# Causal attention on one core: tile 1's mask moved from VectorE to TensorE, and two more PSUM banks for the scores once the last row maxima are out

## What is computed

```python
q, k, v = split(einsum('bsd,ed->bse', x, W_qkv)); q, k = rope(q), rope(k)
scores = where(causal, einsum('bhqd,bhkd->bhqk', q, k) / sqrt(8), -inf)
x = layernorm(x + einsum('bsd,ed->bse', softmax(scores) @ v, W_o))
w = quantize_int4(kernel)                      # round(w / scale), clipped to -8..7, times scale
x = layernorm(x + x @ w + bias + (x @ a) @ b)
```

## Time and profile before

| | us |
|---|---|
| median of 3 runs | 483.12 |
| lowest, highest | 478.73, 485.3 |
| the profiled execution | 482.48 |
| its span, first to last instruction | 480.7 |
| around the span | 1.8 |
| TensorE busy (matmul) | 444.2 |
| VectorE busy | 396.8 |
| ScalarE busy | 311.4 |
| GpSimd busy | 108.1 |
| mean granted TensorE clock | 0.955 |

### The profile page before, as it was taken

How to read it: one execution, slowest core, us unless ns; L and a number is a source line. 1 busy time by engine, 2 the same in 40 slices (tenths; PEclk the granted TensorE clock), 3 DMA queues, 4 the chain that set the end, 5 groups by cost and what they waited for, 6 DMA issues and landing times.

```text
span 480.7 us, 8224 instructions
## 1 busy us (share of the span) xinstructions
PE 444.2 (92%) x2914; PEld 200.1 (42%) x2914; DVE 396.8 (83%) x827; ACT 311.4 (65%) x630; POOL 108.1 (22%) x178
## 2 busy tenths in 40 slices
PE   4988799699799999999999999999999999999972
PEld 2445454334343344343434543434344434434542
DVE  1789689789989999999889999998999989933466
ACT  2324467278067868778778786767786788689610
POOL 8543511201100030020303311030002002442343
PEclk9999879899969999999999999999999999999975
DMA  7322211110000001110000011100000000000001
GB/s 240 143 89 89 91 39 54 54 54 24 3 0 2 1 14 55 55 54 14 3 2 3 14 55 55 54 11 1 1 2 3 1 3 2 3 24 1 22 1 44
DMA packets 11576, 16.54 MB, mean 34 GB/s; under 512 B 1820, under 2 KB 6700, under 8 KB 11536
## 3 DMA queue, kind: packets, MB, share of 16 engines
q1 hardware_dynamic: 10448, 15.75, 9.2%
q0 software_dynamic: 1088, 0.28, 0.3%
HBM read 10.37 MB, written 5.24 MB: 32 GB/s over the span
## 4 chain that ended last, share of the span: by engine, by line
PE 72%; DVE 10%; issue 9%; ACT 4%; POOL 2%; DMA 2%; SPq 0%; POOLq 0%; DVEq 0%; ACTq 0%
PE sT L1110 26%; PE oP L1125 23%; PE ring L1068 13%; DVE pmax L896 8%; ACT probs L814 3%; PE sT L1035 2%; PE ring L1134 1%; DMA qS<-mrows 1%; PE oP L1035 1%; PE sT L1050 1%; PE ring L1154 1%; DMA a_sb<-in_L_ffn_a_dram 1%; DVE summed L870 1%; POOL rstd L715 1%; POOL probs L740 1%
## 5 line engine op out<-in xcount | busy, mean ns | idle before, releaser
L814 ACT ACTIVATE probs<-sT 128x512 f32<-128x512 f32 (+2 forms) x576 | 285.9, 581 | 92.8 <-PE sT L1110 91.6
L896 DVE TENSOR_REDUCE pmax<-ring 128x2 f32<-128x1024 f32 (+2 forms) x212 | 248.7, 1220 | 29.4 <-PE ring L1068 26.4
L1110 PE MATMUL sT<-qS,kS 64*128 64x512 f32 (+3 forms) x648 | 193.1, 423 | 6.4 <-ACT vP L772 2.8
L1068 PE MATMUL ring<-kS,qS 64*128 64x512 f32 (+3 forms) x640 | 152.9, 428 | 7.6 <-DVE pmax L896 5.7
L1110 PEld LDWEIGHTS sT<-qS,kS 64*128 64x128 f32 x648 | 97.2, 191 | 128.3 <-ACT probs L814 107.6
L1125 PE MATMUL oP<-probs,vP 128*9 128x512 f32 (+3 forms) x1296 | 146.7, 532 | 2.0 <-POOL probs L740 1.9
L1068 PEld LDWEIGHTS ring<-kS,qS 64*128 64x128 f32 x640 | 71.0, 190 | 51.3 <-DVE pmax L896 27.4
L870 DVE CUSTOM_DVE_ANT_0 summed<-ring,tail_mask 128x128 bf16<-128x128 f32 (+3 forms) x192 | 81.5, 486 | 8.1 <-PE ring L1068 7.5
L740 POOL TENSOR_SCALAR_AFFINE_SELECT probs<-probs 128x512 f32<-128x512 f32 x64 | 40.2, 634 | 199.1 <-ACT probs L814 198.9
L749 POOL DMA_DIRECT2D qS<-mrows x34 | 19.7, 582 | 98.5 <-DVE mrows L916 94.6
L1125 PEld LDWEIGHTS oP<-probs,vP 128*9 128x9 f32 x1296 | 20.4, 88 | 42.3 <-issue 23.2
(11 more groups left out here) (126 smaller groups left out, 209.1 us busy)
## 6 DMA issues: line engine op xcount, KB each, us to landing
qS<-q_parts SPq DMA_DIRECT2D x52, 64.0 KB
kS<-k_parts SPq DMA_DIRECT2D x52, 64.0 KB
cs<-rope_tables_dram SPq DMA_DIRECT2D x4, 512.0 KB, 7.0
q_parts<-qp SPq DMA_DIRECT2D x4, 512.0 KB, 2.8
k_parts<-kp SPq DMA_DIRECT2D x4, 512.0 KB, 3.0
x_sb<-in_L_attn_x_dram SPq DMA_DIRECT2D x4, 256.0 KB, 6.0
out_dram<-rot SPq DMA_DIRECT2D x2, 256.0 KB, 2.3
qS<-mrows POOLq DMA_DIRECT2D x30, 8.0 KB, 1.8
```

Source lines behind the costliest of these rows:

```text
L814: nc.scalar.activation(probs[:, J % PRING, heads[0]:heads[-1] + 1:2, lo:hi], sT[:, at % SBANKS, 0:len(heads) * (hi - lo)].rearrange("p (h ...
L896: nc.vector.tensor_reduce(dst, src, AX.X, ALU.max).then_inc(unit_free, 1)
L1068: last = nc.tensor.matmul(ring[:, slot_of(e), hl, at:at + w], qS[rows, b, c, hp, ii * TOK:(ii + 1) * TOK], kS[rows, b, kk, hp, 0:w], start ...
L1110: last = nc.tensor.matmul(sT[:, at % SBANKS, x * w:(x + 1) * w], kS[rows, b, j // TPC, hp, (j % TPC) * TOK:(j % TPC + 1) * TOK], qS[rows, ...
```

## The change

1. Own units are masked by VectorE only if they are "01", "02", "2" or "3" of a task from 4 on. ("11", None) gets TensorE's mask in every task, and then the one plain reduction.
2. After the "M" event of the last task (16), the ring's slot that doesn't hold these rows is given to the scores: its two banks join the three of `sT`, first in the rotation, and the sets go round five banks. The other slot's two banks are used singly by the ring events that are left (O and POST). Which bank a set gets and which set had it before is worked out in advance (`BANK`, `HAD`).
3. The planner's costs follow: 0.15 instead of 0.113 us in each plain maxima reduction, 0.24 instead of 0.13 us in each masked one, TensorE's mask 0.3 us dearer, and five banks and two single ring banks after the last M.

```diff
-VECTOR_MASKS = range(NC, len(TASKS))
+def vector_masked(n, unit):
+    return n >= NC and unit[0] in ("01", "02", "2", "3")
...
-    key = (c, first, end, n in VECTOR_MASKS)
+    key = (c, first, end, g > 0)
...
-            if masked and n not in VECTOR_MASKS:
-                end = self.whole(2 * (0.03 + len([x for x in masked if x is not None]) * TOK * self.COLUMN) + self.SWITCH, 0.0)
+            if masked and not vector_masked(n, unit):
+                end = self.whole(2 * (0.03 + len([x for x in masked if x is not None]) * TOK * self.COLUMN) + self.SWITCH + 0.3, 0.0)
...
             self.ready = self.ready[:e[0]] + (self.dve + self.LANDING,) + self.ready[e[0] + 1:]
+            if e[0] == len(TASKS) - 1:
+                self.banks = (self.ring[0],) * 2 + self.banks
+                self.ring = (self.ring[1],) * 2
...
 def maxima_time(n, unit):
-    if unit[0] == "keys" or n not in VECTOR_MASKS:
-        return 0.113 + 2 * width(n, unit) / 960
-    return sum(2 * (0.13 + p[3] / 960) for p in products(n, unit)[0])
+    if not vector_masked(n, unit):
+        return 0.15 + 2 * width(n, unit) / 960
+    return sum(2 * (0.24 + p[3] / 960) for p in products(n, unit)[0])
...
-Course.A_PE = acc(Course.A, lambda x: pair_cost([p[3] for p in products(*x)[0] for _ in range(2)]) + (0.0 if x[1][0] == "keys" or x[0] in VECTOR_MASKS else 0.3))
+Course.A_PE = acc(Course.A, lambda x: pair_cost([p[3] for p in products(*x)[0] for _ in range(2)]) + (0.0 if x[1][0] == "keys" or vector_masked(*x) else 0.6))
...
+LAST_ROWS = UNIT["M", len(TASKS) - 1]
+SLOT, BEFORE = {}, {}
+for e, u in UNIT.items():
+    if u <= LAST_ROWS:
+        SLOT[e], BEFORE[e] = ((u - 1) % 2, 0), u - 2
+    else:
+        SLOT[e], BEFORE[e] = ((LAST_ROWS - 1) % 2, (u - LAST_ROWS - 1) % 2), max(LAST_ROWS, u - 2)
+GIVEN = LAST_ROWS % 2
...
+BANK, HAD, free, last = [], [], list(range(SBANKS)), {}
+for e in SCHEDULE:
+    if e == ("M", len(TASKS) - 1):
+        free = [SBANKS, SBANKS + 1] + free
+    if e[0] == "S":
+        BANK.append(free[0])
+        HAD.append(last.get(free[0]))
+        last[free[0]] = SET[e[1:]]
+        free = free[1:] + free[:1]
...
+        def ring_bank(e):
+            return ring[:, SLOT[e][0], SLOT[e][1], :]
+
+        def score_bank(at):
+            return sT[:, BANK[at], :] if BANK[at] < SBANKS else ring[:, GIVEN, BANK[at] - SBANKS, :]
...
         def slot_taken(pe, e):
-            if UNIT[e] > 2:
-                pe.wait_ge(*RELEASE[UNIT[e] - 2])
+            if BEFORE[e] > 0:
+                pe.wait_ge(*RELEASE[BEFORE[e]])
...
-                if kind != "keys" and n in VECTOR_MASKS:
+                if vector_masked(n, unit):
                     masked_max(n, unit)
...
-                if n in VECTOR_MASKS:
+                if vector_masked(n, unit):
                     masked = None
...
-                if at >= SBANKS:
-                    pe.wait_ge(exp_done, at - SBANKS + 1)
+                if HAD[at] is not None:
+                    pe.wait_ge(exp_done, HAD[at] + 1)
+                elif BANK[at] >= SBANKS:
+                    pe.wait_ge(*RELEASE[LAST_ROWS - 1])
```

More of the change, by code:

```diff
@@ L540, in slot_of @@
         def slot_of(e):
-            return (UNIT[e] - 1) % 2
+            return SLOT[e][0]
+        def ring_bank(e):
+            return ring[:, SLOT[e][0], SLOT[e][1], :]
+        def score_bank(at):
+            return sT[:, BANK[at], :] if BANK[at] < SBANKS else ring[:, GIVEN, BANK[at] - SBANKS, :]
         RELEASE = {}
@@ L814, in exponentials @@
                 nc.scalar.activation(probs[:, J % PRING, heads[0]:heads[-1] + 1:2, lo:hi],
-                                     sT[:, at % SBANKS, 0:len(heads) * (hi - lo)].rearrange("p (h s) -> p h s", h=len(heads)), ACT.Exp,
+                                     score_bank(at)[:, 0:len(heads) * (hi - lo)].rearrange("p (h s) -> p h s", h=len(heads)), ACT.Exp,
                                      scale=float(DK) ** -0.5).then_inc(exp_done, 1)
@@ L938, in normalise @@
                 dve.wait_ge(unit_done, UNIT[e])
-                o = ring[:, slot_of(e), 0, lo:hi].rearrange("p (t h r) -> p t h r", t=end - first, r=VW)
+                o = ring_bank(e)[:, lo:hi].rearrange("p (t h r) -> p t h r", t=end - first, r=VW)
                 nc.vector.reciprocal(rsum[:, first:end, :], o[:, :, :, DK]).then_inc(rs_done, 1)
@@ L952, in post @@
                 dve.wait_ge(unit_done, UNIT[e])
-                src = ring[:, slot_of(e), 0, lo:hi]
+                src = ring_bank(e)[:, lo:hi]
                 if k == 2:
@@ L1109, in scores_t @@
                     rows = slice(HALF * hl, HALF * (hl + 1))
-                    last = nc.tensor.matmul(sT[:, at % SBANKS, x * w:(x + 1) * w], kS[rows, b, j // TPC, hp, (j % TPC) * TOK:(j % TPC + 1) * TOK],
+                    last = nc.tensor.matmul(score_bank(at)[:, x * w:(x + 1) * w], kS[rows, b, j // TPC, hp, (j % TPC) * TOK:(j % TPC + 1) * TOK],
                                             qS[rows, b, c, hp, lo:hi], start=True, stop=True)
@@ L1133, in token_rows @@
                 for t in range(*tiles(n)):
-                    last = nc.tensor.transpose(ring[:, slot_of(e), 0, t * TOK:(t + 1) * TOK], oT[:, n % 2, t * TOK:(t + 1) * TOK], ident[:, :])
+                    last = nc.tensor.transpose(ring_bank(e)[:, t * TOK:(t + 1) * TOK], oT[:, n % 2, t * TOK:(t + 1) * TOK], ident[:, :])
                 last.then_inc(unit_done, 1)
@@ L1138, in post @@
                 e, c, i = ("POST", n, k), TASKS[n][1], turn(n)[0]
-                slot = slot_of(e)
                 slot_taken(pe, e)
@@ L1149, in post @@
                 for t in range(*tiles(n)):
-                    to, cols = ring[:, slot, 0, t * TOK:(t + 1) * TOK], slice(t * TOK, (t + 1) * TOK)
+                    to, cols = ring_bank(e)[:, t * TOK:(t + 1) * TOK], slice(t * TOK, (t + 1) * TOK)
                     if k == 2:
```

## The result

The changed kernel takes 491.59 us (median of 4 runs, 491.14 to 492.9); the kernel before, run beside it, took 484.21 us (median of 4, 478.73 to 487.47). The ratio is 1.0172, with a 95% interval of 1.0122 to 1.0223. So it is some 8 us slower, where 480.5 us was forecast, a gain too small to be told from no change. 491.59 also lies outside the range of 473.0 to 488.5. The profiled execution took 491.14 us with a span of 489.4.

What follows compares the result with a forecast made beforehand. Neither VectorE nor TensorE alone was taken as bound, but TensorE's order with its waits. Masks +1.3, banks -2.3, tail -1.0, planner's costs 0 gave -2.0 us: 482.48 to 480.5 us, 8-in-10 range 473 to 488.5.

Steps and rivals of the forecast that it cites:

- The planner's costs: Whole order rewritten by dearer planner constants: taken as 0, with about 4 us on either side.
- 38 equal periods: Chain's periods of about 2.58 us; each 0.1 us longer or shorter would make 3.8 us.
- Rival 4: New order outweighs both parts, by 3.8 us either way: 476.7 or 484.3 us; chance 0.15, evenly on both sides.
- Rival 1: Tile 1's masks stand on TensorE's path and nothing comes back: 487.7 us, slower; chance 0.20.
- the order decided: Sign of being wrong: task 16's M more than 4 us from 424 us means the order, not the mask.
- 15 plain reductions with four outputs: Sign of being right: plain 1024-element reductions number 15, one per task up to 14, instead of 4.
- ScalarE's idle time: Sign of being right: after the last M, it falls from 5.3 to about 3 us per 26 us.
- Part 1, masks: Tile 1's mask moved to TensorE in 11 units: +1.3 us, between -2.5 (VectorE bound) and +5.2 (TensorE bound).
- Part 2, banks: Five score banks after the last M: -2.3 us, from fewer split steps in about 8 wide steps after 424 us.
- the whole 5.3 us: Ceiling of the banks' gain after 424 us: ScalarE's idle time, at which ScalarE becomes the bound.
- The tail: GpSimd's last masks might be issued before task 14's rstd: -1.0 us, between 0 and -1.9.
- the 1.9 us of before: TensorE's idle time near the end, waiting for GpSimd's last masks behind task 14's rstd; 1.9 us gain at most.

Runs made afterwards that it cites:

- e3: The changed planner's order with the masks and three score banks of the kernel before; ratio to the kernel before 1.0277.
- e7: The changed kernel, masks and five banks included, but planned with the old cost constants; ratio to the kernel before 0.9985.
- e1: The kernel before, order and three banks untouched, with tile 1's mask by TensorE in all tasks; 486.58 us, ratio 1.0030.
- e2: The kernel before, order and masks kept, with score sets going round five banks after the last M; 482.18 us, ratio 0.9955.
- e6: e2 with GpSimd's rstd placed at the NORM event, behind its masks of probabilities; ratio to the kernel before 0.9975.
- e16: The changed kernel with task 11's last maxima units and M(11) moved earlier among the same score sets; ratio to the kernel before 1.0264.
- e18: The changed kernel with the edits of both e16 and e17; ratio to the kernel before 1.0158.
- e5: The changed kernel with GpSimd's rstd of every norm at its NORM event, behind the masks of probabilities; ratio to the kernel before 1.0108.
- e14: The kernel before with one event moved: M(11) directly in front of task 11's first score set; ratio to the kernel before 1.0079.
- e17: The changed kernel with GpSimd's rstd at the NORM event for all norms but task 13's first, which stays at POST 3; ratio 1.0112.
- e15: e7 with GpSimd's rstd placed at the NORM event, behind its masks of probabilities; ratio to the kernel before 0.9984.

## Why the prediction was wrong

**The step that failed** is "The planner's costs ... I take 0, with about 4 us on either side". Measured alone, with the old masks and banks, the new order is +12 to +13 us (e3), three times the bound. The constants by themselves, with the new masks and banks in kernel and planner, are some 9 us (e7 0.9985 against 1.0172). I had bounded it by the 38 equal periods of the steady stretch, each 0.1 us longer or shorter. The loss doesn't come so: it sits where tasks meet. Read from the value products, the stretch from task 9's first to task 10's is 3.9 us longer than before, from task 10's to task 11's 3.5 us; those from 11's to 12's and 12's to 13's, the steady ones, 0.6 us each. About 3 us more come at the end. An order changes when rows are ready against when they are used, and in these traces a miss cost waits and then 6.8 us at half clock. The bound should have come from such a place.

**Rival 4** (the new order outweighs) named the mechanism and gave 484.3 us at worst; it got the sign's chance even and the size wrong. Rival 1's figure of 487.7 us is nearest to the result but for a reason that isn't so: e1 shows the masks at +1.4 us, 3.5 at most. Of the signs set down, the one for "the order decided" came true, and 15 plain reductions with four outputs are there, as said. But ScalarE's idle time in 26 us behind the last M rose from 5.3 to 7.4 us in the changed kernel, where about 3 was forecast:

```profile
433.00:459.00 26.00, 22.36 (x187) 10.44 (x185) 13.24 (x45) 18.63 (x41) 11.24 (x19) 0.98 0.04 11
```

**Part 1, masks**: forecast +1.3 us, measured +1.4 (ratio 1.003, whose interval of -0.6 to +3.5 us holds nothing as well). So near a hit is luck: the forecast was the middle between -2.5 and +5.2, and e1's trace takes 2.3 to 4.0 us longer to M(16) than the five of its order without the masks. In the changed kernel a unit with its mask lasts from 277.58 to 278.39, 0.81 us, as in the earlier trace rows; the eleven lie between 0.65 and 0.98:

```profile
277.58 0.55 PE L1098 MATMUL ring<-kS,qS 64*128 64x256 f32 x4
278.07 0.39 PE L1109 MATMUL ring<-causal,ident_h 128*128 128x256 bf16 x2
278.39 1.05 PE L1157 MATMUL oP<-probs,vP 128*9 128x512 f32 x8
```

The prediction set 0.47 us, where a half-row product follows, against 0.23, where one over all rows does. But 0.47 was the difference of two whole units and 0.23 the mask products alone. Alone, they take 0.32 us up to the next product in all eleven units, here too (278.07 to 278.39), where a value product over all 128 rows follows. So a price that depends on what follows isn't shown by these two numbers.

**Part 2, banks**: forecast -2.3 us, -2.2 by e2's ratio; right in size, though within an interval of -0.5 to -3.8, and on its profile only 0.8 us can be pointed at. ScalarE's idle time fell only to 4.7 us where about 3 was forecast, so the route by which the gain should come isn't confirmed, and the whole 5.3 us did not come. In the new order the banks gain 3.2 us between last M and last value product (41.5 to 38.3).

**The tail**: forecast -1.0 us, "nothing forces the planner to do it". It didn't: TensorE now waits twice for masks, 2.17 us behind an rstd of task 13 and 1.56 us behind that of task 14. Whether the 1.9 us of before are a gain by themselves stays open: e6 removes them from e2, its ratio is 0.9975 against 0.9955, and its trace is 2.4 us shorter. In the changed order the waits are worth about 5 us (e16 to e18), with the norm kept in time; for e5, without that, the intervals allow no gain as well.

**What stays open.** Which cause holds how much of the 11 us. Task 10's end and task 11's start show 3.5 us, a size that e14 reproduces by a late M; that the sparse order there is the cause is argued from the trace, and the one cure tried (e16) made it worse. The 3.9 us in front of it hold one wait for rows of 0.79 us and otherwise more work in the same stretch (seven score sets and one maxima unit); no run isolates it. The 3 us at the end lie where e17 gains about 5. Why the planner's search prefers these orders, which its own costs must have rated better, wasn't tried. Nor was e7 with e17's edit: e7 shows 4.2 us of waits for masks and e15 3.7 us for the norm, so it may beat e2.

## What to carry to other kernels

A cost constant in a planner is a change of the whole program, and has to be tested alone, under a fixed order and with the old constants, before the parts that it accompanies are judged: here the parts alone came to +1.4 and -2.2 us, near their forecasts, and the new constants cost some 9 us. The bound for such a change doesn't come from the steady stretch but from the joints, where one late producer leaves the busiest engine idle and its clock may fall. A wait seen on the busiest engine in front of an in-order queue is a sure gain only when what is pushed back in that queue has nobody waiting for it either: list both before reordering.

## What the runs showed that I had not expected

- In a single wait of TensorE of 3.05 us the clock falls to half, for 6.8 us (e14). In the changed kernel two waits of 0.62 and 0.67 us, at 324.75 and 326.52, came before the same 6.8 us, and a third of 0.84 lies in their beginning. By an estimate from these rows the clock cost more than the waits: 6.8 us at half are up to 3.4 us of work, and TensorE's idle time after M(11) grew by 1.5 us (0.6 to 2.1).
- The way from an M to its rows' landing takes 3.3 to 4.0 us (331.98 to 335.26 in e14, 320.63 to 324.30 before, 324.14 to 328.17 changed), of which the transfers are 1.7 to 1.8 us from GpSimd's issue. An order that has too little other work for TensorE in that time pays for it.
- Three changed constants don't add: 1.2%, 1.1% and 2.6% alone, 1.7% together.
